# The last tile of a fused attention and feed-forward kernel: first layer in one go, second layer one 128-token chunk at a time

## The reference

```python
# attention part
q = silu(x @ Wq1 @ Wq2);  f = sigmoid(x @ Wk1 @ Wk2);  v = x @ Wv
a = exp(log_sigmoid(f));  k = 1 - a
h = scan over tokens of  h = a * h + k * v
out = q * h;  out = out * rsqrt(mean(out * out) + EPS) * norm_w;  out = out @ Wo
x = x + layernorm(attention(layernorm(x)))
# feed-forward part, 6 blocks of hidden width 1024
for i in range(6):
    h = gelu(x @ W1[i].T + b1[i])
    x = h @ W2[i].T + b2[i] + x
    if i < 5: x = layernorm(x, g[i], b[i])
x = x + layernorm(feed_forward(x))
```

## Time and profile before

| | |
|---|---|
| median of 3 runs | 627.28 us (627.17 to 627.36) |
| the profiled execution's own time | 627.12 us |
| its span, first to last instruction | 625.3 us |
| TensorE busy with matmuls | 618.4 us, 99% |
| VectorE busy | 466.8 us, 75% |
| ScalarE busy | 407.4 us, 65% |
| GpSimd busy | 250.4 us, 40% |
| granted TensorE clock, mean | 0.999 |

### The profile page before, as it was taken

The page is one execution under the profiler, slowest core; times in us unless marked ns, Lnnn a source line. Parts: engine busy times, 40 slices in busy tenths (PEclk is TensorE's granted clock), DMA queues, the critical chain, the costliest instruction groups (busy, mean ns, idle before and its releaser), DMA issues.

```text
span 625.3 us, 8866 instructions
## 1 busy us (share of the span) xinstructions
PE 618.4 (99%) x2893; PEld 516.2 (83%) x2893; DVE 466.8 (75%) x826; ACT 407.4 (65%) x685; POOL 250.4 (40%) x229
## 2 busy tenths in 40 slices
PE   8999999999999999999999999999999999999996
PEld 7888888888888888888888888888888888888886
DVE  5998759986676878677786867867766877675676
ACT  5989986868756665565665556655656665555554
POOL 5585510546625362333532253532344422302133
...
DMA packets 56877, 25.13 MB, mean 40 GB/s; under 512 B 47360, under 2 KB 52864, under 8 KB 56832
## 3 DMA queue, kind: packets, MB, share of 16 engines
...
q10 hardware_dynamic: 2400, 0.52, 0.4%
...
## 4 chain that ended last, share of the span: by engine, by line
PE 89%; POOL 3%; DVE 2%; DMA 2%; ACT 1%; issue 1%; SPq 0%; ACTq 0%; POOLq 0%; DVEq 0%
PE BK L169 45%; PE BK L341 39%; PE BK L291 3%; POOL WL L1099 1%; DMA R<-in_wk 1%; PE BK L232 1%; DMA R<-turns 0%; POOL RS L1233 0%; PE BK L243 0%; PE BK L244 0%; PE BK L252 0%; DMA turns<-TB 0%; ACT R L838 0%; ACTq L999 0%; ACT HH L952 0%
## 5 line engine op out<-in xcount | busy, mean ns | idle before, releaser
L952 ACT ACTIVATE HH<-BK,B 128x512 fp32r<-128x512 f32 x192 | 132.2, 688 | 145.8 <-PE BK L169 138.1
L560 DVE TENSOR_TENSOR HL<-BK,HH 128x512 fp32r<-128x512 f32 x192 | 130.5, 684 | 74.1 <-ACT BK L958 71.4
L169 PE MATMUL BK<-XH,WL 128*128 128x512 f32 x416 | 162.7, 391 | 0.0
L169 PE MATMUL BK<-XL,WH 128*128 128x512 f32 x416 | 162.0, 389 | 0.0
L169 PE MATMUL BK<-XH,WH 128*128 128x512 f32 x416 | 161.9, 389 | 0.0
L341 PE MATMUL BK<-HH,WL 128*128 128x512 f32 x368 | 143.5, 390 | 0.0
L341 PE MATMUL BK<-HH,WH 128*128 128x512 f32 x368 | 143.2, 389 | 0.0
L341 PE MATMUL BK<-HL,WH 128*128 128x512 f32 x368 | 143.2, 389 | 0.0
L958 ACT ACTIVATE BK<-BK,B 128x512 f32<-128x512 f32 x192 | 125.1, 655 | 0.0
L169 PEld LDWEIGHTS BK<-XH,WH 128*128 128x128 f32 x416 | 78.1, 188 | 16.4
L169 PEld LDWEIGHTS BK<-XH,WL 128*128 128x128 f32 x416 | 78.1, 188 | 16.2
...
## 6 DMA issues: line engine op xcount, KB each, us to landing
...
sums<-P SPq DMA_DIRECT2D x40, 8.0 KB, 1.4
...
```

Of the source, the lines that this page charges most:

```text
L169: r = eng.matmul(dst, s, m, start=i == 0, stop=i == len(todo) - 1)
L560: eng.tensor_tensor(HL[:, g % HR, :], bank["mm1", n, j][:, :], HH[:, g % HR, :].bitcast(f32), ALU.subtract).then_inc(S["hlo"], 1)
L952: eng.activation(HH[:, g % HR, :], bank["mm1", n, j][:, :], ACT.Gelu, bias=B1[:, 8 * (n // 4) + j:8 * (n // 4) + j + 1]).then_inc(S["ghi"], 1)
```

## The change

Four things change.

**The last tile.** Its pieces 4 to 7 get places of their own: hidden(n, j) puts them into UH, UL, OH and OL, buffers of the attention part that are free by then. So no ghi or hlo of this tile waits for a second-layer piece of the same tile. mm1(23, 3) to mm1(23, 7) run one behind the other, and last_mm2(c, j) follows chunk by chunk: chunk 0 pieces 0 to 6, chunk 1 pieces 0 to 6, the pieces 7 of both, then chunk 2 and chunk 3 whole. Each chunk waits only for its own pre. The number of matmuls is the same. END[2] and END[3] change banks.

**The last chunk.** Chunks 0 to 2 of batch 3 get z_ve and z_rs on GpSimd in place of z_vs on VectorE. Chunk 3 has no step on GpSimd: VectorE subtracts the mean (z_cn), ScalarE takes the square root of variance plus epsilon (z_sd), VectorE its reciprocal (z_rc), and fin0 follows. The square root needs another function table on ScalarE; sqrt_in loads it ahead of z_ng(3, 2).

**The order of the tail.** On ScalarE, VectorE, GpSimd and SyncE the calls of the last tiles stand in another order (rows below).

**The head.** The lists of all engines for attention and tiles 0 to 4 are written in another order, with other PSUM banks. The loops for tiles 5 to 20 are the same. GpSimd sets its constants first, under one semaphore.

```diff
+STEADY_LAST = (3, 1, 0, 2)
-        END = [BK[4], BK[5], BK[2], BK[3]]
+        END = [BK[4], BK[5], BK[3], BK[2]]
+        def hidden(n, j):
+            if n == 4 * NB - 1 and j >= 4:
+                return ((UH, UL) if j < 6 else (OH, OL))[0][:, j % 2, :], ((UH, UL) if j < 6 else (OH, OL))[1][:, j % 2, :]
+            return HH[:, (8 * n + j) % HR, :], HL[:, (8 * n + j) % HR, :]
...
-            def last_mm2(j, chunks=range(4)):
+            def last_mm2(c, j):
                 pe.wait_ge(S["hlo"], 8 * n + j + 1)
                 pe.wait_ge(S["ghi"], 8 * n + j + 1)
                 if j == 0:
-                    pe.wait_ge(S["pre"], 4)
+                    pe.wait_ge(S["pre"], c + 1)
...
             n = 4 * NB - 1
             for j in range(3):
-                mm1(n, j, (3, 1, 0)[j])
+                mm1(n, j, STEADY_LAST[j])
                 mm2(n - 1, 5 + j)
-            mm1(n, 3, 1)
-            mm1(n, 4, 0)
-            last_mm2(0)
-            last_mm2(1)
-            mm1(n, 5, 1)
-            last_mm2(2)
-            mm1(n, 6, 0)
-            last_mm2(3)
-            mm1(n, 7, 1)
-            last_mm2(4)
-            for j, c in ((5, 0), (6, 0), (5, 1), (7, 0), (6, 1), (7, 1), (5, 2), (6, 2), (7, 2), (5, 3), (6, 3), (7, 3)):
-                last_mm2(j, (c,))
+            for j in range(3, 8):
+                mm1(n, j, STEADY_LAST[j % 4])
+            for c in (0, 1):
+                for j in range(7):
+                    last_mm2(c, j)
+            last_mm2(0, 7)
+            last_mm2(1, 7)
+            for c in (2, 3):
+                for j in range(8):
+                    last_mm2(c, j)
...
-                if g >= HR:
+                if g >= HR and (n < 4 * NB - 1 or j < HR):
                     ve.wait_ge(S["mm2"], g - HR + 1)
...
-            def z_vs(c):
-                ve.wait_ge(S["z_mv"], 4 * t + c + 1)
-                eng.tensor_scalar(VE[:, t, c:c + 1], MV[:, t, c, 1:2], EPS_LN, 1.0,
-                                  ALU.add, ALU.mult).then_inc(S["z_vs"], 1)
+            def z_cn():
+                ve.wait_ge(S["z_mv"], 16)
+                eng.tensor_scalar(END[3][:, 0:256], END[3][:, 0:256], MV[:, 3, 3, 0:1], 1.0,
+                                  ALU.subtract, ALU.mult).then_inc(S["z_cn"], 1)
+            def z_rc():
+                ve.wait_ge(S["z_sd"], 1)
+                eng.reciprocal(RS[:, 3, 3:4], VE[:, 3, 3:4]).then_inc(S["z_rc"], 1)
...
+            def sqrt_in():
+                eng.activation(WARM[:, :], ONE[:, :], ACT.Sqrt)
+            def z_sd():
+                ac.wait_ge(S["z_mv"], 16)
+                eng.activation(VE[:, 3, 3:4], MV[:, 3, 3, 1:2], ACT.Sqrt, bias=EPS[:, :]).then_inc(S["z_sd"], 1)
...
-            away(0, 0); away(0, 1); tokens(0, 0); away(3, 0); away(1, 0); away(1, 1); away(3, 1); stored(0, 0)
-            tokens(1, 1); tokens(3, 3); stored(0, 1); away(2, 0); stored(0, 2); half_tokens(0); half_tokens(1)
-            stored(0, 3); stored(1, 0); stored(1, 1); stored(1, 2); stored(1, 3); stored(2, 0); stored(2, 1)
+            away(0, 0); away(0, 1); tokens(0, 0); away(3, 0); away(3, 1); away(1, 0); away(1, 1); stored(0, 0)
+            tokens(1, 1); tokens(3, 3); away(2, 0); stored(0, 1); stored(0, 2); stored(0, 3); stored(1, 0)
+            half_tokens(0); half_tokens(1); stored(1, 1); stored(1, 2); stored(1, 3); stored(2, 0); stored(2, 1)
```

```diff
-            ... proj(3, 0); mm2(1, 1); mm2(1, 2); mm2(1, 3)
-            turn3(2, 0, 2); proj(3, 1); turn3(2, 1, 0); mm1(1, 5, 1); proj(3, 2); mm2(1, 4); mm1(1, 6, 3); proj(3, 3)
+            mm2(1, 0); mm1(1, 4, 1); v(3, 2, 0); mm2(1, 1); v(3, 3, 3); mm2(1, 2); mm2(1, 3); proj(3, 0); proj(3, 1)
+            turn3(2, 0, 0); mm1(1, 5, 2); proj(3, 2); turn3(2, 1, 3); proj(3, 3); mm2(1, 4); mm1(1, 6, 0); rms(3, 1)
...
-            xlo(0, 1); hlo(3, 1); hlo(3, 2); hlo(3, 3); y(2, 0); y(2, 1); tot2(1); hlo(3, 4); vae(1); tr1(2); red1(2)
+            hlo(3, 2); xlo(0, 0); tot2(1); hlo(3, 3); tr1(2); hlo(3, 4); hlo(3, 5); vae(1); red1(2); xlo(0, 1)
```

More of the change, by code:

```diff
@@ L31 @@
 rms ms mm1 ghi gf hlo mm2 y sum1 tr1 red1 tot1 mub ctr sqr sum2 tr2 red2 tot2 vae rsd rsb nn res swap swap_last pre
-end z_st z_mv z_ve z_rs z_nm z_vs z_ng z_ct fin0 fin1""".split()
+end z_st z_mv z_ve z_rs z_nm z_sd z_rc z_cn z_ng z_ct fin0 fin1""".split()
 class Awaiting:
@@ L363, in _ @@
[L363 to L377, removed]
@@ L383, in _ @@
-            mm2(2, 3); mm1(2, 6, 2); mm1(2, 7, 0); mm1(3, 0, 3); mm2(2, 4); mm2(2, 5); mm1(3, 1, 1); mm1(3, 2, 2)
-            mm2(2, 6); mm2(2, 7); mm1(3, 3, 0); mm1(3, 4, 3); mm2(3, 0); mm2(3, 1); mm1(3, 5, 1); mm1(3, 6, 2)
-            mm1(3, 7, 0); mm2(3, 2); mm2(3, 3); mm2(3, 4)
+                    pe.wait_ge(S["pre"], c + 1)
+                wh, wl = w_ffn(NB - 1, 2048 + 256 * j, 256)
+                hh, hl = (h[:, c * 128:(c + 1) * 128] for h in hidden(n, j))
+                for i, (h, w) in enumerate(((hh, wl), (hh, wh), (hl, wh))):
+                    r = eng.matmul(END[c][:, 0:256], h, w, start=False, stop=(j == 7 and i == 2), skip_group_check=True)
@@ L691, in fin0 @@
                 else:
-                    ve.wait_ge(S["z_ct"], 4 * (t - 2) + c + 1)
-                    ve.wait_ge(S["z_rs"], 4 * t + c + 1)
-                    if t == NT - 1:
-                        ve.wait_ge(S["pre"], 4)
+                    if t == NT - 1 and c == 3:
+                        ve.wait_ge(S["z_cn"], 1)
+                        ve.wait_ge(S["z_rc"], 1)
+                    else:
+                        ve.wait_ge(S["z_ct"], 4 * (t - 2) + c + 1)
+                        ve.wait_ge(S["z_rs"], 4 * t + c + 1)
                     src = R[:, t, c, :] if t == 2 else END[c][:, 0:256]
@@ L773, in _ @@
[L773 to L775 removed]
+            mub(19); ctr(19, 0); ctr(19, 1); tr2(19); hlo(21, 0); hlo(21, 1); y(20, 0); red2(19); y(20, 1); hlo(21, 2)
+            tot2(19); hlo(21, 3); swap(0, 0); swap(0, 1); hlo(21, 4); hlo(21, 5); hlo(21, 6); vae(19); rsb(19)
@@ new lines, in _ @@
+            nn(19, 0); nn(19, 1); hlo(21, 7); xlo(19, 0); swap_last(0); z_st(20, 0); z_mv(20, 0); hlo(22, 0)
+            xlo(19, 1); z_st(20, 1); z_st(20, 2); swap_last(1); y(21, 0); z_mv(20, 1); hlo(22, 1); z_nm(20, 0)
+            z_mv(20, 2); y(21, 1); z_st(20, 3); swap(1, 0); hlo(22, 2); fin0(0, 0); swap(1, 1); hlo(22, 3); hlo(22, 4)
+            z_mv(20, 3); hlo(22, 5); hlo(22, 6); z_st(21, 0); z_mv(21, 0); z_st(21, 1); z_mv(21, 1); z_st(21, 2)
+            z_nm(20, 1); z_mv(21, 2); z_nm(20, 2); hlo(22, 7); hlo(23, 0); z_nm(20, 3); z_nm(21, 0); fin0(0, 2)
@@ new lines, in _ @@
+            hlo(23, 1); z_st(21, 3); y(22, 0); y(22, 1); swap(2, 0); swap(2, 1); z_mv(21, 3); hlo(23, 2); hlo(23, 3)
+            z_nm(21, 1); fin0(1, 0); z_nm(21, 2); hlo(23, 4); hlo(23, 5); hlo(23, 6); hlo(23, 7); z_nm(21, 3)
+            fin0(1, 2); z_st(22, 0); z_st(22, 1); z_mv(22, 0); z_st(22, 2); z_mv(22, 1); z_mv(22, 2); z_st(22, 3)
+            z_st(23, 0); z_mv(22, 3); z_st(23, 1); z_mv(23, 0); fin0(2, 0); fin0(2, 1); z_mv(23, 1); z_st(23, 2)
+            z_mv(23, 2); fin0(2, 2); fin0(2, 3); fin0(3, 0); fin0(3, 1); fin0(3, 2); z_st(23, 3); z_mv(23, 3); z_cn()
@@ L777, in _ @@
+            z_rc(); fin0(3, 3)
         @block.scalar
```

266 lines of the change are left out of this document (131 added, 135 removed).

## The result

The changed kernel takes 628.11 us (median of 19 runs, 627.36 to 628.91), the kernel before 627.09 beside it (626.44 to 627.56). The ratio is 1.0016, 95% interval 1.001 to 1.0022: 1.0 us slower, under the 1.25 us called no change. The range held it; the forecast of 627.4 was 0.7 too low, and it was a sum of two misses of opposite sign.

What follows compares the result with a forecast made beforehand. The prediction took TensorE, busy 618.4 of 625.3 us, as the bound, with two chains of almost one length at the end. Head +0.15 and tail -0.05 gave +0.1 on 627.28: 627.4, range 626.3 to 628.8.

Steps and rivals of the forecast that it cites:

- Where the end comes from: Kernel's end: two chains of almost one length, TensorE then chunk 3's statistics, and batch 2's tokens then GpSimd's list.
- GpSimd's list: Tail, GpSimd up to z_rs(23, 2): seven z_ve, six z_rs and fin1 take 5.7; ends at T0 + 7.2, or 0.4 later.
- T0: Tail, VectorE: the start of z_st(22, 0), put at G + 5.7 = 613.45, against 613.55 before.
- The head: Attention and tiles 0 to 4: rewritten lists cost +0.15 us, with bounds -0.5 and +1.2.
- Gains 0.2 and losses 0.35: Head: little TensorE idle time to win back, 0.2; waits near proj(3, 3) and mm1(4, 0) among the losses; +0.15 in sum.
- ScalarE and the DMAs: Tail: three away2_1 issues at 0.94 each ahead of ghi(23, 5); TensorE waits 0.8, last matmul starts at 620.7.
- G: Tail, ScalarE: the start of ghi(23, 5), taken as 607.75; hlo(23, 5), (6), (7) end at G + 2.55, 3.65, 5.1.
- The rival that the issues collide: Tail, three away2_1 ahead of ghi(23, 5): at 1.2 to 1.4 each, tail costs 0.6 to 1.2; 628.0 to 628.8; chance 0.22.
- the one that they run free: Tail, same DMA issues: at 0.54 each the tail is 0.9 better, 626.4 to 626.6; chance 0.22.
- When batch 2's chain starts: Tail: tokens land at G - 0.45 + 2.63 + 3.12 = G + 5.3, stores issued by then; z_st(22, 0) starts at 613.45.
- The last chunk, the table load: Kernel's end: z_st(23, 3) to last fin0 1.2, not 1.79, but starting later: -0.05; load of 1.28, no drain, costs nothing.
- The rule on issuing engines: Tail, DMAs from ScalarE and SyncE: by the skill's rule the spread gains nothing; the prediction then calls the collision rival likelier.

Runs made afterwards that it cites:

- 625.15 or 625.41: Changed kernel with half_tokens ahead of the stores and z_vs back on VectorE for chunks 0 to 2 of batch 3, timed twice: 625.15 us, again 625.41 us.

## Why the prediction was right, and where it was wrong

**Where the end comes from.** Right: two chains of almost one length, with the tokens of batch 2 and GpSimd's list ahead of z_st(23, 3), and TensorE behind them. Moving pre(3) shows it, and so does the fixed distance from T0 to z_st(23, 3).

**The head.** Wrong. The forecast was +0.15; it was -0.8. The step that failed is "Gains 0.2 and losses 0.35": no wait appeared at proj(3, 3) or mm1(4, 0), and the gain came out of small hand-overs that the text counted as 0.2 and that sum to about 1 in the two traces (the matmuls that waited for UL start 0.4 earlier, at 11.56 and not 11.99, and mm1(23, 3) 1.15; the new head alone has 0.95 there).

**ScalarE and the DMAs.** The size was off, and so was its reason: three issues of 0.67 each, not 0.94 (2.01 in the trace of after). From ghi(23, 5) on the walk held: hlo(23, 5), (6) and (7) ended at G + 2.56, 3.70 and 5.16. TensorE's wait for pieces 5 and 6, forecast as 0.8, was 0.2 in that trace. The rival that the issues collide did not come; the one that they run free came in part. The slow rows that the 0.94 was taken from have something else in them. SyncE's fourth issue and ScalarE's second in the kernel before, and the DMA queue of instructions from 605.4 to 606.6:

```profile
605.36 1.67 SPq L1330 DMA_DIRECT2D turns<-SA  x1
605.87 1.16 ACTq L999 DMA_DIRECT2D turns<-TB  x1
```

```profile
q8 instruction: 1, 0.02, 5.7%
```

A 16 KB instruction fetch ran from 605.48 to 606.57, on top of both. The new head with the old tail has it in the same place (604.43, with issues of 1.46 and 0.95). In the eleven traces in which both queues issue their four DMAs in the new order, without a fetch there, none of the eight issues is over 0.74. No run moves the fetch alone, but over all fourteen traces every issue of more than 1 us from 100 us on has such a fetch over it, except the store told of in the last section.

**When batch 2's chain starts.** This is the step that failed most: the sum "2.63 + 3.12" for the landing of the tokens, with "SyncE's stores ahead of half_tokens are issued by then" as all that the stores could cost. They were issued by then, at 608.1, before the last away2_1 had landed (608.8). But the forecast put T0 at G + 5.7, which would be 611.5 with the measured G = 605.84, and it was 614.2: the last away2_1 landed 3.72 after issue, and half_tokens 5.39 after its own. Without the stores ahead T0 is 611.65, G + 5.73, and the time 1.9 lower. Taking the durations of before for a DMA that now has others ahead of it on its queue was the mistake. What exactly holds up a queue with four more issues isn't settled: most of the data isn't needed for it, and issues, packets and the fetch are not told apart.

**GpSimd's list.** The term was mis-sized. T0 to the end of z_rs(23, 2) was put at 7.2 to 7.6; it was 8.0 (614.2 to 622.24). Six z_rs were priced by the step from one z_rs to the next, 0.52, but five of them have a z_ve behind them and then take 0.63 to 0.72. The rows of before had said so: the prediction saw 3.4 by its steps take 3.83, and put the 0.4 on as it was, where a list of 5.7 would make it 0.7. Undoing the three moved z_ve gives 1.1 back, with and without the late tokens.

**The last chunk, the table load.** Right: 1.33 from z_st(23, 3) to the last fin0, forecast 1.2 within 1.0 to 1.4, and it starts behind GpSimd's list, so it was worth nothing that the times show. The 0.6 that it was to save is too much: beside the power in the same order it saves 0.2. The load cost 1.28 with no drain (618.77, then 620.06), as the rows said, where the Trainium skill ("ScalarE: Activation LUTs", section "What ACT_TABLE_LOAD costs") has 2.66 in all.

**The rule on issuing engines.** The Trainium skill ("DMA: Bandwidth & Descriptors", section "Issuing engines are not separate DMA queues") says a second issuing engine saves only sequencer time. The last issue ends 0.9 earlier with two engines, and the time is 1.1 lower. But the last landing is only 0.1 to 0.5 earlier, since each DMA lands 2.0 after issue from one engine and 2.5 to 3.3 from two; the rest of the 1.1 is in the landing of half_tokens. The prediction's reading, that the spread "gains nothing", is near the truth for the landings of the away DMAs and wrong for the time.

**Sum.** -0.8 for the head, +1.9 for the order of half_tokens and the stores, +1.1 for z_ve on GpSimd. What else the new tail does (the last tile in one go, the swaps and DMAs earlier, the square root) gave back what lies between 626.13, new head and old tail, and 625.15 or 625.41: 1.0 or 0.7. Together +1.2 to +1.5, for 1.0 measured. Which part of the rest gave how much wasn't tried.

**Luck.** The number came out well for reasons that the prediction didn't have. Two of its own signs of being wrong came: ghi(23, 5) before 607, and z_st(22, 0) waiting for half_tokens, by 2.56. No rival had the stores in it, and the loss they make was hidden by a head that was to lose 0.15 and won 0.8, and by what else the tail gave back.
